# Block two of an attention and expert kernel: the combination's matmuls in six pieces, and an earlier split of causal q and k

## What is computed

```python
t = t + _L0_ffn_ref(...)          # routed: zeros.at[token_buf].add(yb), the "combination"
x = _from_tokens(t, x)
# block two, local attention: rows of 16 positions, 12 heads of 16
x = x + _L1_conv_ref(_ln_c(x), ...)
# block two, causal attention over an image's positions, then the second experts
t = _to_tokens(x)
t = t + _L1_ffn_ref(_ln_t(t), ...)
```

## Time and profile before

| what | us |
|---|---|
| runs before the change | 1264.54, 1266.11, 1271.5 (median 1266.11) |
| the profiled execution, its own time | 1268.68 |
| its span, first to last instruction | 1266.9 |
| of it TensorE busy | 1035.6 (82%) |
| VectorE busy | 738.9 (58%) |
| ScalarE busy | 488.2 (39%) |
| GpSimd busy | 321.6 (25%) |
| first to last combination matmul (L1906) | 516.8 to 895.4 |

### The profile page before, as it was taken

One profiled execution on the slowest core, in us unless ns is written; L12 is line 12 of the kernel. 1 busy time (PEld: TensorE's weight loads), 2 busy tenths in 40 slices (PEclk: granted clock), 3 DMA queues, 4 the chain that ended last, 5 costly groups with the idle time before them and its releaser, 6 DMA issues.

```text
span 1266.9 us, 26138 instructions
## 1 busy us (share of the span) xinstructions
PE 1035.6 (82%) x9573; PEld 803.9 (63%) x9573; DVE 738.9 (58%) x2299; ACT 488.2 (39%) x1221; POOL 321.6 (25%) x516
## 2 busy tenths in 40 slices
PE   4899999999998799776787887788877745899992
PEld 3677776777776355565575666566655535888882
DVE  6586686686584144255767776768677653233334
ACT  1453453453452122042555455555456421112210
POOL 0000000000000820364636455354110121222222
PEclk8999999999998899887999999999998767999996
DMA  9052152242243999000000000000000006888885
GB/s 351 18 142 88 53 141 82 59 141 77 64 141 114 291 418 376 13 1 1 1 2 1 18 1 19 1 19 8 11 18 1 18 22 236 288 292 284 301 288 168
DMA packets 69040, 144.61 MB, mean 114 GB/s; under 512 B 4896, under 2 KB 55360, under 8 KB 66656
## 3 DMA queue, kind: packets, MB, share of 16 engines
q1 hardware_dynamic: 64352, 132.75, 31.6%
q0 software_dynamic: 4608, 10.79, 2.6%
HBM read 97.22 MB, written 46.30 MB: 113 GB/s over the span
## 4 chain that ended last, share of the span: by engine, by line
PE 37%; DVE 26%; issue 22%; ACT 6%; POOL 5%; DMA 4%; another core or an unknown queue 1%; POOLq 0%; DVEq 0%; ACTq 0%; SPq 0%
DVE neg_max L705 5%; PE bank L1769 4%; PE bank L560 3%; PE bank L605 3%; PE bank L627 3%; PE bank L799 3%; PE bank L1906 3%; PE bank L669 2%; PE bank L1797 2%; DVE R L678 2%; POOL sorted_x L1052 2%; PE bank L806 2%; DMA R<-in_ffn_gu 2%; POOL token_y L1083 2%; ACT R L734 2%
## 5 line engine op out<-in xcount | busy, mean ns | idle before, releaser
L734 ACT ACTIVATE R<-bank,neg_max 128x128 f32<-128x128 f32 (+2 forms) x576 | 189.1, 404 | 143.0 <-DVE neg_max L705 142.9
L1040 POOL TENSOR_SCALAR R<-cf,ids_rel 128x128 bf16<-128x128 f32 x256 | 169.4, 678 | 0.3
L605 PE MATMUL bank<-cf,R 128*128 128x128 f32 x864 | 136.5, 282 | 27.8 <-ACT R L743 14.4
L705 DVE TENSOR_REDUCE neg_max<-bank 128x2 f32<-128x352 f32 (+2 forms) x216 | 129.9, 609 | 33.5 <-PE bank L588 28.0
L605 PEld LDWEIGHTS bank<-cf,R 128*128 128x128 f32 x864 | 96.7, 144 | 45.6 <-ACT R L734 31.0
L992 POOL TENSOR_TENSOR rstd<-mean_var,cf 128x2 f32<-128x2 f32 x24 | 4.7, 194 | 461.5 <-DVE mean_var L862 461.5
L757 ACT ACTIVATE R<-bank 128x1024 bf16<-128x1024 bf16 x72 | 70.5, 1021 | 77.6 <-PE bank L560 77.2
L1769 PE MATMUL bank<-R 64*116 64x256 f32 (+1 forms) x512 | 97.9, 400 | 0.0
L560 PE MATMUL bank<-cb,R 128*128 128x128 bf16 x1008 | 70.7, 234 | 27.2 <-DVE R L545 27.1
L560 PEld LDWEIGHTS bank<-cb,R 128*128 128x128 bf16 x1008 | 65.3, 106 | 35.3 <-DVE R L545 26.0
L1684 DVE TENSOR_TENSOR R<-R,bank 128x384 f32<-128x384 f32 x48 | 26.6, 554 | 104.0 <-ACT R L1218 98.7
(11 more groups left out here) (250 smaller groups left out, 1942.1 us busy)
## 6 DMA issues: line engine op xcount, KB each, us to landing
R<-in_ffn_w SPq DMA_DIRECT2D x48, 864.0 KB, 5.5
sorted_x<-cmp SPq DMA_DIRECT2D x8, 4128.0 KB, 16.4
R<-in_ffn_gu SPq DMA_DIRECT2D x16, 1392.0 KB, 18.9
R<-in_ffn_dn SPq DMA_DIRECT2D x16, 768.0 KB, 16.3
xs_words<-sorted_x SPq DMA_DIRECT2D x48, 129.0 KB
R<-token_y SPq DMA_DIRECT2D x8, 384.0 KB, 6.6
rows<-R SPq DMA_DIRECT2D x8, 224.0 KB, 2.3
out_x<-x_all SPq DMA_DIRECT2D x16, 96.0 KB, 2.5
```

The costliest lines, as they stand in the source:

```text
L605: ins = nc.tensor.transpose(PT[u % 2][:, at + g * P:at + (g + 1) * P], probs[:, u % 3, g * kw + c0:g * kw + c0 + P], ident)
L705: nc.vector.tensor_reduce(neg_max[:, u % 4, 0:g], score_bank(a, u)[:, 0:g * kw].rearrange("p (g k) -> p g k", g=g), AX, ALU.max, negate=Tr ...
L734: ins = nc.scalar.activation(probs[:, u % 3, g * kw:(g + 1) * kw], score_bank(a, u)[:, g * kw:(g + 1) * kw], ACT.Exp, bias=neg_max[:, u % ...
L1040: ins = nc.gpsimd.tensor_scalar(comb_s[:, t, j, :], cst("iota_tok"), ids_rel[:, j:j + 1], None, ALU.is_equal)
```

## The change

The 32 steps of the combination are cut at 0, 4, 9, 15, 20, 26, 32 in place of 0, 10, 20, 32, and stand in `extra[1]` to `extra[6]` in place of `extra[1]` to `extra[3]`. `w_head` moves from `(7, "transposed")` to `(8, "transposed")`, in front of `m_head`. On VectorE `combine` moves from `between[3]` to `between[6]` and `w_norm` from 5 to 7; the six split steps move from 4 to 8 to 3, 4 and 5, two in each. The amount of work is the same.

```diff
                 if i + 2 < B:
-                    between[3].append(lambda: combine(i + 2))
-                    between[5].append(lambda: w_norm(i + 2))
+                    between[6].append(lambda: combine(i + 2))
+                    between[7].append(lambda: w_norm(i + 2))
...
-                    for k, n in ((4, 0), (5, 1), (6, 2), (7, 3), (8, 4), (8, 5)):
+                    for k, n in ((3, 0), (3, 1), (4, 2), (4, 3), (5, 4), (5, 5)):
                         between[k].append(split[n])
...
-                n = 2 * NPAIR // 3
+                at = [0, 4, 9, 15, 20, 26, 2 * NPAIR]
 
                 def piece(k):
                     if k == 1 and i >= 0:
                         causal_qkv(i)
                     if i + 2 < B:
-                        c_comb(i + 2, (k - 1) * n, k * n if k < 3 else 2 * NPAIR)
-                for k in range(1, 4):
+                        c_comb(i + 2, at[k - 1], at[k])
+                for k in range(1, 7):
                     extra[k] = lambda k=k: piece(k)
-                if i + 2 < B:
-                    extra[(7, "transposed")] = lambda: w_head(i + 2)
-                if i >= 1:
-                    extra[(8, "transposed")] = lambda: m_head(i - 1)
+
+                def heads():
+                    if i + 2 < B:
+                        w_head(i + 2)
+                    if i >= 1:
+                        m_head(i - 1)
+                extra[(8, "transposed")] = heads
```

## The result

| kernel | median us | ratio to before, with its 95% interval |
|---|---|---|
| before | 1266.66 | 1 |
| after | 1290.04 (1285.74 to 1298.02) | 1.0185 [1.0148, 1.0222] |
| after again (e9_after_again; before 1268.74 beside it) | 1290.71 | 1.0191 [1.0166, 1.0216] |

The change costs 22 to 24 us where 10.3 were forecast: slower, as predicted, but by more than twice as much, and outside the range. The profiled executions show less of it. That of after is 17.1 us over that of before (1285.74 and 1268.68), because it is the fastest of its four and the one of before lies 2 us above its median. Their spans are 1283.9 and 1266.9 us.

What follows compares the result with a forecast made beforehand. TensorE was taken as nearest the limit, taking turns with VectorE and ScalarE in W3's second half. W0 +1.5, W1 and W2 -1.0, W3 to W6 +10.4, W7 -0.6 make +10.3 on 1266.11: 1276.4 us, range 1267 to 1285.

Steps and rivals of the forecast that it cites:

- The chain to `w_head`: W0 to W6: `w_head` can start 4.68 us after group 4's transposes start, so TensorE waits 2.4 us.
- the walk: Prediction's step-by-step path through the engines' queues at measured prices, all windows, without clock falls: +10.3 us.
- The held windows: W3 to W6, where the stores hold VectorE early: +2.6 us each, taken as +10.4 together.
- W0, W1 and W2: Windows where the stores don't hold VectorE: W0 +1.5 us, W1 and W2 -0.5 each.
- The early split and W7: W1 to W7: no wait for line 545 left; W7, without combination, -0.6 us, bounds 0 and -1.4.
- Sum. +1.5 - 1.0 + 10.4 - 0.6 = +10.3: Whole kernel: W0, W1 with W2, W3 to W6 and W7 added as one chain, counted in full, +10.3 us.
- the fall of the clock as a rival: Front half of W3 to W6: thinned TensorE work drops to half clock, +4 to +8 us on top; chance 0.16.

Runs made afterwards that it cites:

- e9_after_again: The changed kernel itself, unaltered, run once more and more often beside later runs: 1290.71 us, ratio to before 1.0191.
- e10: Changed kernel with the same normalisation written once more, into a buffer nothing reads, in front of `w_norm`: ratio to before 1.0224.
- e3: Changed kernel with `m_rows` and its wait for the stores moved late, from u = 0 to u = 3 on VectorE: 1268.59 us, ratio to before 1.0011.
- e5: Changed kernel with 26 extra matmuls before `w_head` in W0 to W6, none in front: 1286.55 us, ratio to before 1.0114.
- split-only kernel: Kernel before with only the six split steps moved to u = 3, 3, 4, 4, 5, 5: 1277.62 us, ratio to before 1.0069.

## Why the prediction was right in direction and wrong in size

**The chain to `w_head`: right.** Forecast 2.4 us of waiting in W1 to W6; measured 2.2 in all seven, and the waits grow by what is added to the chain (e10). From group 4's transposes to `w_head` the walk had 4.68 us; the trace of after has 4.71, 4.68 and five times 4.5 to 4.6.

**The held windows: right.** +2.6 forecast, +2.3 measured in the three windows at full clock; with VectorE not held they lose 3.7 us (e3), forecast 4.3.

**W0, W1 and W2: right at full clock only.** In W0 the second denominators come 6.45 us after group 4's transposes (558.20 to 564.65) in place of 4.97: +1.48, forecast +1.5; the half clock behind them makes the stage 3.6 longer. -0.5 was forecast for W1 and W2 each. W2 gives -0.4 with fillers (e5); W1 with them is 0.5 longer than before as a stage, though from group 4's transposes to its end it is 0.3 shorter. In the changed kernel both are longer.

**The early split and W7: right.** No wait for line 545 is left in the windows; W7 -0.6 (-1.4 in the second trace).

**The step that failed: "Sum. +1.5 - 1.0 + 10.4 - 0.6 = +10.3".** It had no term for the clock. By stage, in us over before, from the traces:

| stages | forecast | after | after again (e9) | head's fillers (e5) |
|---|---|---|---|---|
| W0 | +1.5 | +3.6 | +3.4 | +2.4 |
| W1 and W2 | -1.0 | +3.9 | +3.7 | +0.2 |
| W3 to W6 | +10.4 | +11.7 | +13.8 | +11.6 |
| W7 | -0.6 | -0.6 | -1.4 | -0.7 |
| sum | +10.3 | +18.6 | +19.5 | +13.5 |
| W0 to W6 at half clock (before: 17) | | 42 | 48 | 27 |

The excess over the forecast, 8 to 9 us, lies most of all in W0 to W2 and comes with 24 to 31 us more at half clock. Taken from the start of `w_head` to the end of the window, 6.68 us at full clock (for W0 6.74, with fillers), falls there cost 1.0, 1.95, 1.3 and 1.5 us in W0 to W3 of after, 5.7 together; in the front of W3 another 0.9 or so. The rest, up to the 22 to 24 of the medians, fits the profiled executions: the one of before is 2 us slower than its median, those of after 2 and 4 us faster than theirs.

I had the fall of the clock as a rival at 0.16, priced at +4 to +8, and put into "exactly the front half of W3 to W6". There it fell in W3 of both traces and in W6 of the second, and cost at most 1 us each time, because a wait behind it took it up. What cost time was the fall at the new wait of 2.2 us, in W0 to W3 and any other window, which the head's fillers undo: they give back some 10 us of the 24 by the ratios, those in front none. The place mattered for the chance: I had argued that W3 holds 1.00 through pauses of up to 1.44 us, and never set my own forecast wait of 2.4 beside the 1.81 after which C2 loses its clock. That row was in hand and said that a longer pause might not be safe. That the price of +4 to +8 comes near the excess of 8 to 9 in the traces is luck: it was worked out for another place. The Trainium skill ("TensorE: Matmul & The Clock Gate", HAM oscillation), cited in the prediction, says that idle stretches between bursts halve the clock. The measured time went that way, and the shares of 0.94 and 0.90 in W2 and W3, 1.00 in before, agree with it; W4 to W6, at 1.00 with the same waits, show that the wait alone doesn't settle it.

What is left after the fillers, 13.5 us in the trace and 13 to 14 by the ratios, is 3 above the walk's 10.3: about 1 each in W0, in W1 and W2, and in W3 to W6, where W3 still has a share of 0.95 and is 3.7 us longer than before. How much of it is the fillers' own cost isn't shown. Nor is it shown why the clock falls behind the same wait in W1 to W3 and not in W4 to W6 of one execution. It isn't tied to those windows: in the second trace W6 falls too. The other runs of the changed kernel, with mean shares of 0.920 to 0.931 over the whole span against the profiled one's 0.935, took 1289.6 to 1298.0 us, which suggests more falls in them.

## What to carry to other kernels

When work is spread to fill an engine's pauses, look first at what waits for its last piece: here a chain of 4.7 us over VectorE and GpSimd, hidden while the work ended early, became the wait of the whole window. Price each new TensorE wait twice, once for its length and once for the half clock that may follow it. Take the second price as a range, here from nothing to 2 us a window, wherever the forecast pause is longer than a pause after which the trace already shows a fall and the work right behind it is what the stage waits for. And before spreading cover work, find the wait that it covers and move that wait first: a spread over five pieces, ended one group earlier and with the stores' wait moved, beats the kernel before by 1.4%.

## What the runs showed of the hardware

Extra matmuls that nothing needs made a kernel faster: 26 of 128x192 in each of seven waits of 2.2 us took some 10 us off (ratio to before 1.0191 without, 1.0114 with). In before, where W2 to W6 keep the full clock, 16 of them per window cost 0.4% (1.0042).

A pause of 2.2 to 2.4 us was enough for the granted clock to fall to 1.2 GHz (in W1 of after during it, in W3 of the split-only kernel behind it), but not each time: in W4 to W6 of after and W3 to W6 of the kernel with rows late the same pause left it at 2.4.

What a fall costs depends on what stands behind it. Behind `w_head`, where the stage waits for TensorE, it cost 1.95 us in W1 of after (8.63 us to the end of the window, 6.68 with fillers). In the front of W3, with a wait behind it, it cost 0.9. In C2 of before it cost nothing: that stage lasts 30.08 us, as does C1, which has no fall.
